# Attention scores in 64x64 array tiles on 48 stacked rows, and a step written out in slots

## The chip, the cores and the metric

The kernel runs on one core of a Trainium2 chip. The metric is the device time of one execution in microseconds (us), the median of several runs. The engines work from queues of their own and meet at semaphores: PE (TensorE, matrix products), DVE (VectorE), ACT (ScalarE), POOL (GpSimd) and SP (SyncE, which here only issues DMAs).

## The reference

One post-norm transformer layer in float32 on x of 8 batches, 256 tokens, 128 features: attention with 16 heads of 8 dimensions and a sliding window of 128 keys, then a layer norm, then a mixture of 8 experts of which each token takes its best 2, then a layer norm.

```python
q, k, v = (to_heads(a) for a in jnp.split(x @ w_qkv.T, 3, axis=-1))   # 16 heads of 8
att = jnp.einsum('bhqd,bhkd->bhqk', q, k) / sqrt(8)
att = where((j <= i) & (j >= i - 127), att, -inf);  att = softmax(att)
x = layernorm(x + (att @ v) @ w_out.T)
probs = softmax(x @ router_w);  top_p, top_e = top_k(probs, 2)
y = sum over the two experts e of top_p * (gelu(x @ w_in[e] + b_in[e]) @ w_out[e] + b_out[e])
x = layernorm(x + y)
```

## The kernel before

**Exact scores from bfloat16.** Queries and keys are projected in float32, one batch at a time (`project_qk`, L926), and each value is split into three bfloat16 parts. ACT copies the first part out of PSUM (`take_top`, L550); DVE takes the rest by subtraction, the middle part by a conversion and the last by another subtraction (`split_rest`, L671 to L676). SP writes the parts to memory and reads them back stacked on partitions (`write_parts`, `stack`), so that one bfloat16 product over 72 rows (9 products of parts, each of 8 dimensions) gives a score. A batch has two stacks of 8 heads each, and there are buffers for two batches.

**Two passes over the scores.** The first pass finds each row's largest score. In the first tile of 128 queries a mask goes into PSUM by a product with the identity (L942), then one product a head (L945). In the second tile, for 2 heads at a time, there is a mask (L955) and per head two products of 64 queries by 192 keys, in the two column halves of the array (L960). DVE takes the maxima (L743, L748). They are split into three parts (`split_max`, L685 to L691), turned on PE (L1001), copied by ACT (L482) and written by a DMA into three rows below the stacked queries, which makes 75 rows. The second pass (`turned_scores`, L977 and L978) gives the scores turned and with the maximum taken off: per head 256 and 128 columns. ACT takes the exponential of one head at a time out of one of two banks (L474), POOL masks (L432, L436), and PE weighs the values in four column tiles of 32 (`weigh_values`, L992, L994).

**What follows in a step.** The output is turned (L1008), divided by its sums (DVE L698, L706), turned (L1014), projected (L1020), added to x and normed (DVE), turned again (L1026), and gives router logits (L1032).

**The order.** It is written out by hand. `step` treats one batch's first pass together with the second pass of the batch before and the tail of the two before that, in four quarters `g` of four heads. A first stretch of steps and the last two are written out; the steps between run in a hardware loop (`Fori`), where addresses and semaphore values come from registers. The experts follow, in 4 chunks of 512 tokens: a first layer (L1043, three products of 512 columns), gelu on ACT (L574), a second layer (L1051), and DVE adds the share (L813). Their first units are interleaved with the last batch's attention.

## Time and profile before

| | us |
|---|---|
| median of 3 runs | 224.44 (224.05 to 225.66) |
| the profiled execution, its own time | 223.83 |
| its span in the trace | 221.8 |

The span is the time between the first and the last instruction of the trace; the profiled execution has 2.0 us outside it. On the page a group of instructions has its busy time and the mean duration of one. Matrix products are pipelined: two that follow each other start closer together than one lasts, so what a product costs its engine is read from the difference of two starts. An idle time is put down to what ended it.

### The profile page before, as it was taken

The page shows a single profiled execution, that of the slowest core. Times are in us where ns is not written, and L with a number is a line of the kernel's source. Part 1 is how long each engine was busy: PE and PEld are TensorE (multiplying, and loading weights), DVE is VectorE, ACT ScalarE, POOL GpSimd, SP SyncE. Part 2 cuts the span into 40 slices and gives each one's busy share as a digit, 9 for nine tenths or more (in the row PEclk, how much of TensorE's full clock was granted, in tenths as well). Part 3 has the DMA queues.
Part 4 walks back from the last instruction along what each step waited for, and adds up shares of the span by engine and source line. Part 5 has one row for each costly group of instructions (what it writes and reads, how often), then busy time and mean ns, then how long its engine had stood idle before and what let it go on. Part 6 is the DMA issues. An engine that isn't in the chain of part 4 may idle for free.

```text
span 221.8 us, 5963 instructions
## 1 busy us (share of the span) xinstructions
PE 203.4 (92%) x1906; PEld 135.9 (61%) x1908; DVE 182.9 (82%) x522; ACT 116.7 (53%) x270; POOL 89.2 (40%) x166
## 2 busy tenths in 40 slices
PE   7786999989999999999999999989999899999960
PEld 4332446555565565565566566656688798989950
DVE  6664655789979989989989998977899888988883
ACT  2200106647557557557557566769445756374530
POOL 7230003375445635635635536478244211422103
PEclk9997559999999999999999999999999999999996
DMA  4947751542633533533533431000000001000011
GB/s 113 282 117 240 202 148 46 151 147 77 170 120 104 163 110 99 162 104 99 160 104 99 158 104 29 5 26 3 0 4 0 0 3 45 7 24 24 3 47 47
DMA packets 20391, 19.66 MB, mean 89 GB/s; under 512 B 1609, under 2 KB 17937, under 8 KB 20369
## 3 DMA queue, kind: packets, MB, share of 16 engines
q1 hardware_dynamic: 20180, 19.30, 29.4%
q8 instruction: 12, 0.20, 0.4%
q14 instruction: 10, 0.08, 0.1%
q10 hardware_dynamic: 189, 0.09, 0.1%
HBM read 13.94 MB, written 5.24 MB: 86 GB/s over the span
## 4 chain that ended last, share of the span: by engine, by line
PE 63%; DVE 17%; issue 7%; ACT 4%; DMA 4%; POOL 1%; SPq 1%; DVEq 1%; POOLq 0%; ACTq 0%
PE bank L1051 12%; PE bank L1043 9%; PE bank L960 7%; PE bank L977 5%; PE bank L992 4%; PE bank L955 3%; PE bank L942 3%; PE bank L945 3%; PE bank L926 3%; PE bank L1089 3%; DMA ks<-k_scratch 2%; DVE rest L671 2%; DVE neg_max L748 2%; PE bank L978 2%; DVE parts L676 2%
## 5 line engine op out<-in xcount | busy, mean ns | idle before, releaser
L474 ACT ACTIVATE probs<-bank 128x384 f32<-128x384 f32 x128 | 60.0, 496 | 34.7 <-PE bank L978 32.5
L432 POOL TENSOR_SCALAR_AFFINE_SELECT probs<-probs 128x1024 f32<-128x1024 f32 x32 | 35.7, 1116 | 67.8 <-ACT probs L474 67.8
L813 DVE SCALAR_TENSOR_TENSOR x_rows<-bank,gate_c,x_rows 128x128 f32<-128x128 f32 (+1 forms) x128 | 36.6, 343 | 5.3 <-PE bank L1051 4.2
L748 DVE TENSOR_REDUCE neg_max<-bank 128x2 f32<-128x384 f32 x64 | 33.5, 546 | 3.4 <-PE bank L960 3.1
L1051 PE MATMUL bank<-w_out_sb,hid 128*128 128x128 f32 x256 | 34.2, 277 | 1.0 <-DVE x_rows L813 1.0
L1051 PEld LDWEIGHTS bank<-w_out_sb,hid 128*128 128x128 f32 x256 | 32.6, 191 | 3.4 <-DVE x_rows L813 1.4
L574 ACT ACTIVATE hid<-bank,b_in_sb 128x512 f32<-128x512 f32 x32 | 21.9, 687 | 22.4 <-PE bank L1043 22.3
L977 PE MATMUL bank<-qs,ks 75*128 75x256 bf16 x128 | 33.4, 279 | 0.1
L743 DVE TENSOR_REDUCE neg_max<-bank 128x4 f32<-128x512 f32 x32 | 21.9, 685 | 8.8 <-PE bank L945 8.1
L978 PE MATMUL bank<-qs,ks 75*128 75x128 bf16 x128 | 26.9, 218 | 0.0
L436 POOL TENSOR_SCALAR_AFFINE_SELECT probs<-probs 128x512 f32<-128x512 f32 x32 | 24.2, 756 | 0.0
L960 PE MATMUL bank<-ks,qs 72*64 72x192 bf16 x256 | 24.1, 271 | 0.0
L992 PE MATMUL bank<-probs,v 128*32 128x256 f32 x256 | 20.4, 391 | 0.0
L977 PEld LDWEIGHTS bank<-qs,ks 75*128 75x128 bf16 x128 | 12.8, 100 | 11.0 <-ACT probs L474 0.7
L955 PE MATMUL bank<-mask_second,ident_bf 128*128 128x256 bf16 x64 | 18.6, 290 | 0.8 <-DVE neg_max L748 0.3
L960 PEld LDWEIGHTS bank<-ks,qs 72*64 72x64 bf16 x256 | 9.3, 111 | 11.9 <-issue 10.3
L942 PE MATMUL bank<-mask_first,ident_bf 128*128 128x512 bf16 x32 | 13.2, 412 | 3.5 <-DMA ks<-k_scratch 3.5
L1089 PE MATMUL bank<-idle_rows 128*128 128x512 bf16 x50 | 14.6, 445 | 1.8 <-DVE idle_rows L791 1.4
L1043 PE MATMUL bank<-x_hi,w_in_lo 128*128 128x512 f32 (+1 forms) x32 | 15.3, 478 | 0.0
L563 ACT ACTIVATE v<-bank 128x64 f32<-128x64 f32 x32 | 4.6, 234 | 17.5 <-PE bank L932 17.5
L945 PEld LDWEIGHTS bank<-ks,qs 72*128 72x128 bf16 x128 | 10.6, 103 | 5.0 <-issue 1.4
L945 PE MATMUL bank<-ks,qs 72*128 72x128 bf16 x128 | 13.4, 231 | 0.0
(117 smaller groups left out, 343.8 us busy)
## 6 DMA issues: line engine op xcount, KB each, us to landing
qs<-q_scratch SPq DMA_DIRECT2D x16, 288.0 KB
ks<-k_scratch SPq DMA_DIRECT2D x16, 288.0 KB
q_scratch<-parts SPq DMA_DIRECT2D x8, 192.0 KB, 2.1
k_scratch<-parts SPq DMA_DIRECT2D x8, 192.0 KB, 2.4
x_cols<-x_t SPq DMA_DIRECT2D x8, 128.0 KB, 2.6
x_rows<-x SPq DMA_DIRECT2D x8, 128.0 KB, 2.2
k_scratch<-parts SPq DMA_DIRECT2D x8, 128.0 KB, 2.3
out<-y_sb SPq DMA_DIRECT2D x8, 128.0 KB, 1.8
```

Of the source, the lines that this page charges most:

```text
L432: pool.affine_select(out=own, in_=own, compare_op=ALU.is_ge, fill=0.0, base=0, pattern=[[0, 2], [0, 4], [1, P]], channel_multiplier=-1).th ...
L474: nc.scalar.activation(probs[g][:, :, i, :], st_banks(spare)[k % len(st_banks(spare))][:, 0:3 * P].rearrange("p (k c) -> p k c", k=3), ACT ...
L748: nc.vector.tensor_reduce(neg_max[:, 1, 4 * g + 2 * u:4 * g + 2 * u + 2], score_bank[1 + u][:, 0:384].rearrange("p (h c) -> p h c", h=2), ...
L813: nc.vector.scalar_tensor_tensor(token_rows(c, n), y_bank[e % 4][:, n * E:(n + 1) * E], gate_of(c, n, e), token_rows(c, n), ALU.mult, ALU. ...
L945: last = mm(score_bank[0][:, i * P:(i + 1) * P], q[0:ROWS, h, 0:P], k[0:ROWS, h, 0:P], start=False, stop=True, skip_group_check=True)
L955: mm(edges, ident_bf[:, :], mask_second[:, :, :].unsqueeze(1).to_broadcast([P, 2, 2, 64]), start=True, stop=True)
L960: last = mm(bank_u[lo:lo + 64, i * 192:(i + 1) * 192], q[0:ROWS, h, P + lo:P + lo + 64], k[0:ROWS, h, lo:lo + 192], start=False, stop=True ...
L977: mm(out_bank[:, 0:T], k[0:KROWS, h, 0:P], q[0:KROWS, h, :], start=True, stop=True)
L978: mm(out_bank[:, T:T + P], k[0:KROWS, h, P:T], q[0:KROWS, h, P:T], start=True, stop=True).then_inc(st_ready, 1)
L992: last = mm(o_bank[rows, t * T:(t + 1) * T], v, probs[g][:, 0:2, j, :], start=s == 0, stop=s == 1, skip_group_check=True)
L1043: last = mm(hid_bank[e % 2][:, :], w[:, e, :], xx[:, cols], start=i == 0, stop=i == 2)
L1051: last = mm(y_bank[e % 4][:, n * E:(n + 1) * E], hid[e % 2][:, n * P:(n + 1) * P], w_out_sb[:, e, :], start=True, stop=True)
```

## The change

**Scores.** Of the nine products of parts six are kept (`PRODUCTS`), so a score needs 48 rows. An even and an odd head now lie side by side, at partitions 0 and 64. Both passes use products of at most 64 rows and 64 output partitions. The four of one pair of heads (two heads, two halves of the queries or keys) lie in the four quarters of the array, and the two heads write to different banks. The masks are made in the same shape, four products to a job. The second pass does a pair of heads at once, into one buffer of two banks, and ACT takes one exponential of 768 columns for it (L417) where it took two of 384. The maxima of all 16 heads are split in one go, by two DVE instructions, turned in one go and written by two DMAs.

**Splitting.** The first part is taken off inside PSUM by a product with minus the identity (`subtract_top`); ACT makes the middle part (`take_middle`), DVE the last (`take_low`).

**Loads.** There are four stacks. The five writes of a batch go out as their parts are ready, and a batch is projected 14 slots ahead. All of x in rows comes in one load, and most of x in columns is loaded after the first two stacks.

**Order.** The loops are gone. A batch has 8 slots, in which the constants say which piece is done; 75 slots are written out for every engine.

```diff
-BLK = PARTS * D
-ROWS = PARTS * BLK
+PRODUCTS = ((0, 1), (0, 0), (0, 2), (1, 0), (1, 1), (2, 0))
+ROWS = len(PRODUCTS) * D
+KROWS = ROWS + PARTS
...
-LOAD_WARM_UP = 7
-WARM_UP = 34
+LOAD_WARM_UP = 8
+WARM_UP = 44
...
+STACKS = 4
+TURN_MAX, VALUES, S2, PV = 8, 12, 11, 15
+COPY_O, TURN_O, TURN_ATTN, PROJECT_OUT, TURN_X1, LOGITS = 22, 23, 25, 26, 30, 31
+PROJECT_QK = -14
+LAST_S1, LAST_S2 = 8 * B - 1, 8 * B - 1 + S2
+SCORE_JOBS = {0: (False, 0), 1: (True, 0), 2: (True, 2), 4: (False, 4), 5: (True, 4), 6: (True, 6)}
+JOBS = 2 * len(SCORE_JOBS)
...
-                q0, k0 = par * PARTS * E, par * (2 * PARTS - 1) * E
-                sp.wait_ge(part_low, b.times(1, 1))
-                sp.dma_start(q_scratch[q0:q0 + PARTS * E, :].rearrange("(a r) t -> r a t", a=PARTS),
-                             parts[par][:, :, 0, :]).then_inc(scratch_written[par], 16)
-                sp.dma_start(k_scratch[k0:k0 + PARTS * E, :].rearrange("(a r) t -> r a t", a=PARTS),
-                             parts[par][:, :, 1, :]).then_inc(scratch_written[par], 16)
-                sp.dma_start(k_scratch[k0 + PARTS * E:k0 + (2 * PARTS - 1) * E, :]
-                             .rearrange("(a r) t -> r a t", a=PARTS - 1),
-                             parts[par][:, 0:PARTS - 1, 1, :]).then_inc(scratch_written[par], 16)
...
+            def stack(b):
+                sp.wait_ge(scratch_written[b % 2], 80 * (b // 2 + 1))
+                if b >= STACKS:
+                    sp.wait_ge(st_ready, PAIRS * (b - STACKS + 1))
+                for i, operand in enumerate((qs, ks)):
+                    for r in range(2):
+                        sp.dma_start(operand[b % STACKS][64 * r:64 * r + ROWS, :, :],
+                                     scratch[b % 2, i, :, r, :].rearrange("a (n t) -> a n t", n=PAIRS)).then_inc(stacked[b % STACKS], 16)
+            def stack_max(b):
+                sp.wait_ge(max_copied, b + 1)
+                for r in range(2):
+                    sp.dma_start(qs[b % STACKS][64 * r + ROWS:64 * r + KROWS, :, :],
+                                 max_t[r * PARTS * PAIRS:(r + 1) * PARTS * PAIRS, :]).then_inc(max_stacked[b % STACKS], 16)
...
+            write_parts(0)
+            sp.wait_ge(ones_ready, 1)
+            stack(0)
+            write_parts(1)
             sp.wait_ge(ones_ready, 2)
+            stack(1)
+            sp.dma_start(x_t_sb[:, 2 * T:B * T], x_t[:, 2 * T:B * T]).then_inc(x_t_loaded[2], 16)
+            sp.dma_start(wout_sb[:, :], wout_t).then_inc(out_w_loaded, 16)
+            sp.dma_start(router_sb[:, :], router_w).then_inc(moe_w_loaded, 16)
+            sp.dma_start(b_in_sb[:, :], b_in_t).then_inc(moe_w_loaded, 16)
+            sp.dma_start(x_sb[:, :, :], x.rearrange("(n p) e -> p n e", p=P)).then_inc(x_loaded, 16)
+            sp.wait_ge(ones_ready, STACKS)
...
+            def exponentials(b, p):
+                g = p // 2
+                if p % 2 == 0 and b:
+                    act.wait_ge(pv_done, QUADS * (b - 1) + g + 1)
+                act.wait_ge(st_ready, PAIRS * b + p + 1)
+                two = slice(2 * (p % 2), 2 * (p % 2) + 2)
+                nc.scalar.activation(probs[g][:, :, two, :].rearrange("p k j c -> p j k c"),
+                                     st[:, :, 0:3 * P].rearrange("p j (k c) -> p j k c", k=3), ACT.Exp, scale=SCALE).then_inc(exp_done, 1)
...
+            def take_middle(b):
+                act.wait_ge(part_rest, b + 1)
+                nc.scalar.activation(parts[b % 2][:, 1, :, :], projection_bank(b)[:, :].rearrange("p (a t) -> p a t", a=2), ACT.Copy).then_inc(part_mid, 1)
...
+                for offset, piece in ((TURN_MAX, copy_max), (TURN_ATTN, copy_attention), (PROJECT_QK, take_top), (PROJECT_QK + 1, take_middle),
+                                      (VALUES, pad_v), (COPY_O, copy_output), (TURN_X1, copy_x1), (LOGITS, copy_logits)):
...
-            def split_rest(b, in_use=True):
-                p = parts[b.parity]
-                dve.wait_ge(part_top, b.times(1, 1))
-                if in_use:
-                    dve.wait_ge(part_low, b.times(1))
-                nc.vector.tensor_tensor(rest[:, :, :], misc[0][:, :].rearrange("p (a t) -> p a t", a=2), p[:, 0, :, :],
-                                        ALU.subtract).then_inc(part_rest, 1)
-                dve.wait_ge(part_rest, b.times(1, 1))
-                nc.vector.tensor_copy(p[:, 1, :, :], rest[:, :, :]).then_inc(part_mid, 1)
-                dve.wait_ge(part_mid, b.times(1, 1))
-                nc.vector.tensor_tensor(p[:, 2, :, :], rest[:, :, :], p[:, 1, :, :], ALU.subtract).then_inc(part_low, 1)
...
+            def take_low(b):
+                p = parts[b % 2]
+                dve.wait_ge(part_mid, b + 1)
+                nc.vector.tensor_tensor(p[:, 2, :, :], projection_bank(b)[:, :].rearrange("p (a t) -> p a t", a=2), p[:, 1, :, :],
+                                        ALU.subtract).then_inc(part_low, 1)
...
+            def split_max(b):
+                part = max_parts[b % 2]
+                upper = upper_half(part[:, :, :, :, :])
+                dve.wait_ge(maxima, JOBS * (b + 1))
+                nc.vector.tensor_tensor(part[:, :, :, 1, :], part[:, :, :, 0, :], upper[:, :, :, 0, :], ALU.subtract).then_inc(max_rested, 1)
+                dve.wait_ge(max_rested, b + 1)
+                nc.vector.tensor_tensor(part[:, :, :, 2, :], part[:, :, :, 1, :], upper[:, :, :, 1, :], ALU.subtract).then_inc(max_split, 1)
...
+                if slot == LAST_S1 + 1:
+                    split_weights()
+                    route_shift(EARLY, B // 2 - 1)
+                if slot == LAST_S1 + 2:
+                    choose(EARLY, 1)
...
+            def subtract_top(b):
+                pe.wait_ge(part_top, b + 1)
+                mm(projection_bank(b)[:, :], minus_bf[:, :], parts[b % 2][:, 0, :, :], start=False, stop=True, skip_group_check=True).then_inc(part_rest, 1)
...
+            def scores(b, second, pair, job):
+                q, k = qs[b % STACKS], ks[b % STACKS]
+                heads, width = (2, 192) if second else (4, P)
+                if job % JOBS == 0:
+                    pe.wait_ge(stacked[b % STACKS], 64 * (b // STACKS + 1))
+                for r in range(2):
+                    if job + r >= 3:
+                        pe.wait_ge(maxima, job + r - 2)
+                    bank = score_bank[(job + r) % 3][:, 0:heads * width].rearrange("p (h c) -> p h c", h=heads)
+                    rows = slice(64 * r, 64 * r + 64)
+                        cols = slice(64 * half, 64 * half + 64)
+                        if second:
+                            at = bank[cols, :, :].rearrange("p h (a c) -> p h a c", a=3)[:, :, 0:3:2, :]
+                            mask = edges[rows, 0:2, :].unsqueeze(1).to_broadcast([64, heads, 2, 64])
+                        elif half:
+                            at = bank[cols, :, 64:P]
+                            mask = edges[rows, 1, :].unsqueeze(1).to_broadcast([64, heads, 64])
+                        else:
+                            at = bank[cols, :, :]
+                            mask = edges[rows, 1:3, :].rearrange("p a c -> p (a c)").unsqueeze(1).to_broadcast([64, heads, P])
+                        mm(at, ident_bf[rows, 64 * r:64 * r + 64], mask, start=True, stop=True)
+                for i in range(heads):
+                    for r in range(2):
+                        rows = slice(64 * r, 64 * r + ROWS)
+                        bank = score_bank[(job + r) % 3]
+                        for half in range(2):
+                            lo = 64 * half
+                            if second:
+                                keys, queries = slice(lo, lo + 192), slice(P + lo, P + lo + 64)
+                            else:
+                                keys, queries = slice(0, 64 + lo), slice(lo, lo + 64)
+                            last = mm(bank[lo:lo + 64, i * width:i * width + keys.stop - keys.start], q[rows, pair + i, queries], k[rows, pair + i, keys],
+                                      start=False, stop=True, skip_group_check=True)
+                        if i == heads - 1:
+                            last.then_inc(scores_ready, 1)
...
+            def turned_scores(b, p):
+                q, k = qs[b % STACKS], ks[b % STACKS]
+                if p == 0:
+                    pe.wait_ge(max_stacked[b % STACKS], 32 * (b // STACKS + 1))
+                if b or p:
+                    pe.wait_ge(exp_done, PAIRS * b + p)
+                for kt in range(2):
+                    for half in range(2):
+                        for r in range(2):
+                            rows, cols = slice(64 * r, 64 * r + KROWS), slice(64 * half, 64 * half + 64)
+                            at = kt * P + 64 * half
+                            last = mm(st[cols, r, kt * T:kt * P + T], k[rows, p, at:at + 64], q[rows, p, kt * P:T], start=True, stop=True)
+                last.then_inc(st_ready, 1)
...
+            for slot in range(LAST_S2 + 1):
+                n = pair_at(slot)
+                if n is not None:
+                    turned_scores(*n)
+                elif slot < S2:
+                    keep_warm(2)
+                n = jobs_at(slot)
+                if n is not None:
+                    scores(*n)
...
+                b = batch_at(slot, PROJECT_QK)
+                if b is not None:
+                    if b == 2:
+                        pe.wait_ge(x_t_loaded[2], 16)
+                        pe.wait_ge(part_low, 2)
+                    elif b < 5:
+                        pe.wait_ge(max_copied, b - 2)
+                    else:
+                        pe.wait_ge(attn_copied, b - 4)
+                    project_qk(b)
+                b = batch_at(slot, PROJECT_QK + 1)
+                if b is not None:
+                    subtract_top(b)
```

The places where the order of the instructions matters here are two. On PE in the loop, at the start of a quarter (`bank` is a bank of PSUM, `qs` and `ks` the stacked queries and keys), there stood before:

```order
L941 REGISTER_ALU
L942 MATMUL bank<-mask_first,ident_bf 128x512
L945 MATMUL bank<-ks,qs 128x128 x4
L975 REGISTER_ALU
L977 MATMUL bank<-qs,ks 128x256
L978 MATMUL bank<-qs,ks 128x128
L953 REGISTER_ALU
L955 MATMUL bank<-mask_second,ident_bf 128x2x2x64
L960 MATMUL bank<-ks,qs 64x192 x4
```

Now a slot of the steady part (the third of a batch) reads, up to the projections that follow:

```order
L938 MATMUL st<-qs,ks 64x256 [waits exp_done]
L938 MATMUL st<-qs,ks 64x256 x3
L938 MATMUL st<-qs,ks 64x128 x4
L910 MATMUL score_bank<-edges,ident_bf 64x2x2x64 [waits maxima]
L910 MATMUL score_bank<-edges,ident_bf 64x2x2x64
L910 MATMUL score_bank<-edges,ident_bf 64x2x2x64 [waits maxima]
L910 MATMUL score_bank<-edges,ident_bf 64x2x2x64
L921 MATMUL score_bank<-ks,qs 64x192 x8
L997 MATMUL misc<-wout_sb,attn_t 128x128 [waits attn_copied]
L997 MATMUL misc<-wout_sb,attn_t 128x128
L868 MATMUL misc<-x_t_sb,wqkv_sb 128x256 [waits attn_copied]
L868 MATMUL misc<-x_t_sb,wqkv_sb 128x256
```

The turned scores moved to the head of the slot; they come as eight small products behind one wait for the exponential of the pair before, and the projections follow behind waits for ACT. On SP at the start (`x_t` is x in columns, with 1536 columns for the batches from the third on) there stood before:

```order
L286 DMA b_in_sb<-b_in_t 128x8
L287 DMA x_t_sb<-x_t 128x1536
L290 DMA b_out_rows<-b_out 24x1x128 x3
L248 DMA q_scratch<-parts 128x3x256
L250 DMA k_scratch<-parts 128x3x256
L252 DMA k_scratch<-parts 128x2x256
L266 DMA qs<-q_scratch 72x1x2048
L266 DMA ks<-k_scratch 72x1x2048
```

Now, from the second batch's last write on:

```order
L228 DMA scratch<-parts 128x2x256 [waits part_low]
L238 DMA qs<-scratch 48x2048 [waits scratch_written1,ones_ready]
L238 DMA qs<-scratch 48x2048
L238 DMA ks<-scratch 48x2048 x2
L261 DMA x_t_sb<-x_t 128x1536
L262 DMA wout_sb<-wout_t 128x128
L263 DMA router_sb<-router_w 128x8
L264 DMA b_in_sb<-b_in_t 128x8
L265 DMA x_rows<-x 128x16x128
L212 DMA scratch<-parts 128x3x256 [waits part_top,stacked0,ones_ready]
```

The load of the 1536 columns moved behind the writes and the stacks of two batches.

## Rows read from the trace of the kernel before

**Rows 1.** Page, busy us with share of the span, and count, of each engine.

```profile
PE 203.4 (92%) x1906; PEld 135.9 (61%) x1908; DVE 182.9 (82%) x522; ACT 116.7 (53%) x270; POOL 89.2 (40%) x166
```

**Rows 2.** Stretches of 10 us: busy (count) of each engine, clock, DMA share, GB/s.

```profile
20.00:30.00 10.00, 9.67 (x57) 4.49 (x57) 6.38 (x15) 0.95 (x5) 0.00 (x0) 0.50 0.56 159
...
100.00:110.00 10.00, 9.64 (x118) 5.78 (x116) 9.64 (x23) 6.46 (x18) 5.98 (x8) 1.00 0.43 127
```

**Rows 3.** Page, the chain that ended last: its shares by engine.

```profile
PE 63%; DVE 17%; issue 7%; ACT 4%; DMA 4%; POOL 1%; SPq 1%; DVEq 1%; POOLq 0%; ACTq 0%
```

**Rows 4.** Timeline (start us, us, engine, line, op): TensorE around two heads' scores.

```profile
88.79 0.38 PE L942 MATMUL bank<-mask_first,ident_bf 128*128 128x512 bf16 x1
...
89.01 0.39 PE L945 MATMUL bank<-ks,qs 72*128 72x128 bf16 x4
...
89.23 0.27 PE L977 MATMUL bank<-qs,ks 75*128 75x256 bf16 x1
...
89.40 0.27 PE L955 MATMUL bank<-mask_second,ident_bf 128*128 128x256 bf16 x1
...
89.60 0.36 PE L960 MATMUL bank<-ks,qs 72*64 72x192 bf16 x4
...
89.89 0.28 PE L977 MATMUL bank<-qs,ks 75*128 75x256 bf16 x1
```

**Rows 5.** Timeline, TensorE, and a group (mean ns): weighing the values, and what follows.

```profile
91.31 0.42 PE L992 MATMUL bank<-probs,v 128*32 128x256 f32 x4
...
L992 PE MATMUL bank<-probs,v 128*32 128x256 f32 x256 | 20.4, 391 | 0.0
...
129.13 0.40 PE L994 MATMUL bank<-probs,v 128*32 128x128 f32 x8
129.46 0.71 PE L1020 MATMUL bank<-wout_sb,attn_t 128*128 128x128 f32 x4
```

**Rows 6.** Groups by line and shape (count, busy us, mean ns, idle before): VectorE and ScalarE.

```profile
L474 ACT ACTIVATE probs<-bank 128x384 f32<-128x384 f32 x128 | 60.0, 496 | 34.7 <-PE bank L978 32.5
...
L748 DVE TENSOR_REDUCE neg_max<-bank 128x2 f32<-128x384 f32 x64 | 33.5, 546 | 3.4 <-PE bank L960 3.1
...
L743 DVE TENSOR_REDUCE neg_max<-bank 128x4 f32<-128x512 f32 x32 | 21.9, 685 | 8.8 <-PE bank L945 8.1
...
L676 DVE TENSOR_TENSOR parts<-rest,parts 128x512 bf16<-128x512 f32 x8 | 10.4, 1302 | 0.3
...
L691 DVE TENSOR_TENSOR max_parts<-max_rest,max_parts 128x16 bf16<-128x16 f32 x16 | 8.0, 497 | 0.5
...
L685 DVE CAST max_parts<-neg_max 128x16 bf16<-128x16 f32 x16 | 6.0, 374 | 0.7
...
L550 ACT ACTIVATE parts<-bank 128x512 bf16<-128x512 f32 x8 | 4.8, 597 | 8.7 <-PE bank L926 8.7
```

**Rows 7.** Timeline: two projections of queries and keys, four rounds apart.

```profile
34.26 1.08 PE L926 MATMUL bank<-x_t_sb,wqkv_sb 128*128 128x256 f32 x4
...
98.15 1.08 PE L926 MATMUL bank<-x_t_sb,wqkv_sb 128*128 x4
```

**Rows 8.** Timeline and DMA issues (KB each, median us to landing): the start.

```profile
13.91 0.78 SPq L266 DMA_DIRECT2D ks<-k_scratch  x1
...
18.79 0.39 PE L942 MATMUL bank<-mask_first,ident_bf 128*128 128x512 bf16 x1 [2.76 <-DMA ks<-k_scratch]
...
33.42 0.27 PE L977 MATMUL bank<-qs,ks 75*128 75x256 bf16 x1
...
q_scratch<-parts SPq DMA_DIRECT2D x8, 192.0 KB, 2.1
...
x_t_sb<-x_t SPq DMA_DIRECT2D x1, 768.0 KB, 5.8
```

**Rows 9.** Timeline, and group: the first second layer, and the splitting of the weights.

```profile
157.64 1.16 PE L1051 MATMUL bank<-w_out_sb,hid 128*128 128x128 f32 x8
...
L788 DVE TENSOR_TENSOR w_in_lo<-w_in_sb,w_in_hi 128x1024 fp32r<-128x1024 f32 x1 | 2.0, 1995 | 0.0
```

1154 lines of the change are left out of this document (490 added, 664 removed).

## The prediction

> **What bounds the kernel now.** I read the page's busy times first, then the stretches, the chain of waits, and last the timeline of one quarter of a step. TensorE is busy 92% of the span and VectorE 82% [rows 1]. In the stretches of 10 us in mid-attention TensorE is busy 9.64 and VectorE 9.64, ScalarE 6.46 [rows 2]. So the two lie side by side; the chain has 63% on PE and 17% on DVE [rows 3]. Four rounds of the loop lie between the projections at 34.26 and 98.15 [rows 7], so one step, which is one batch, takes (98.15 - 34.26) / 4 = 16.0 us. I cut the time at three points: the first turned scores at 33.42 [rows 8], the first second layer at 157.64 [rows 9], and the end at 221.8. That makes 33.4, 124.2 and 64.2 us.
>
> **TensorE per batch.** Costs are differences of starts [rows 4]. A first tile of 4 heads takes 89.23 - 88.79 = 0.44, a head's turned scores 89.40 - 89.23 = 0.17, a second tile of 2 heads 89.89 - 89.40 = 0.49. Scores cost 4 x 0.44 + 16 x 0.17 + 8 x 0.49 = 8.4 of the 16.0 us, and all else 7.6. In the second tile the mask's 256 columns need 0.11 at 2.4 GHz and start 0.20 before the products of half width; these need 2 x 192 columns, 0.16, when halves run together, and start 0.29 before the next. So there are 0.09 and 0.13 us at each change of tile shape. Behind the values, whose last 128 columns pass four times in float32, each of two pairs of passes 0.11, it is 129.46 - 129.13 - 0.21 = 0.12 [rows 5]. I take 0.11.
>
> After the change four small products share the array. The trace shows column tiles together: four weighings of 256 columns start within 0.42 - 0.39 = 0.03 us of each other [rows 5]. Row halves together it does not show. Bounds: fully together, a pair's turned scores take 256 + 128 columns = 0.16; not at all, 0.32. I take 0.16, nearest to the column tiles. A first job of 8 heads is 512 columns of mask and 4 x 128, 0.43; a second job of 4 heads 256 + 2 x 192, 0.27. Per batch: 8 x 0.16 + 2 x 0.43 + 4 x 0.27 = 3.2 where 8.4 stood. The subtraction adds 512 columns, 0.21. Projections, turns and values now each leave the 64x64 shape and return: some 18 changes a batch, of which 8 stood around the values and are in the 7.6; 10 x 0.11 = 1.1 more. TensorE's own work: 7.6 + 3.2 + 0.2 + 1.1 = 12.1 us.
>
> The Trainium skill has a rule against such small products (TensorE: Matmul & The Clock Gate, on the gap of two matmuls: "Start-to-start never drops below ≈25 ns however small N is"). The row has four starts in 0.03 us, 10 ns each or less, and speaks against it; with 25 ns the time would be that of the fourth rival.
>
> **VectorE per batch.** It has 0.96 x 16.0 = 15.4 us [rows 2]. The maxima stay: 8 x 0.52 and 4 x 0.69 [rows 6]. Of the three splitting instructions the 1.30 of L676 goes, and another conversion that I leave uncounted. Splitting the maxima took 8 instructions a batch, the first kind 0.37 and the last 0.50 in the mean [rows 6], so 8 x 0.44 = 3.5; now 2 of at most twice that, 0.9. Left: 15.4 - 1.3 - 2.6 = 11.5.
>
> **ScalarE per batch.** 384 columns take 0.50 and 512 take 0.60 [rows 6], 0.8 ns a column, so 768 take 0.82: 6.6 for 8 where 16 x 0.47 = 7.5 stood. The middle part adds 0.60. ScalarE had 0.65 x 16 = 10.3 and has 10.0.
>
> **Why a batch won't take 12.1.** There is one buffer for turned scores: PE may write a pair only when the exponential of the pair before is done. I walked one batch on paper, slot by slot, with these durations and 0.3 from a product's start to its reader. A slot whose TensorE work is short waits for the exponential: turned scores 0.11 + 0.37, exponential 0.82, 0.1 back, 1.4 us, which costs 0.4 in the first slot. With three score banks PE waits for VectorE in three slots, 0.2, 0.3 and 0.5. The subtraction stands one slot behind the projection, and ScalarE's copy (0.60 and 0.3 to reach it) is hidden only by the turned scores: 0.7. The logits wait for a copy behind an exponential and the copy of the output: 0.8. Sum 2.9; about 0.7 of waiting was in the 7.6. So 12.1 + 2.2 = **14.3 us** a batch, against 16.0.
>
> **The start.** First scores come at 18.79 now [rows 8]. Afterwards 46 warm-up products replace 34 and end near 19, about when the first stack is there. Slots 0 to 2 end near 22. Then `project_qk` of the third batch needs the 1536 columns. Their load follows five writes, four reads of 0.78 each to issue, five writes and four reads. The first set is written by 10, landed 2.1 later [rows 8], the reads issued by 15.3; second writes by 18, landed near 20.4, reads issued by 24; then the load, 768 KB, which took 5.8 to land beside others [rows 8]. It can do with 4: **28.5**. PE idles 6 us. Before, TensorE stood still before 18.79 and the stretch from 20 to 30 has clock 0.50, the 1.2 GHz level [rows 2]; I expect it again here. From 28.5: projection 1.8 at that level, copy 0.7, warm-up products and subtraction 1.2, copy 0.7, last part 0.8 with its issue, landing 2.5: 36.4. Four reads to issue, 3.2; behind them on SP the two writes of the first batch's maxima, 1.6, and landing 2: the first turned scores at **43.3**, not 33.4. That is 9.9 lost. If the load takes 5.8 it is 2 more; if 2.5, 1.5 less.
>
> **The middle.** Slots 11 to 15: 5 x 1.4 = 7. Slots 16 to 63, six batches: 85.8. The last two of these have no projection (0.91 + 0.32 + 0.7 of waiting, 3.9 for both), and the first has no tail yet, where turns, logits and their wait would be 2; I take off 5, as VectorE takes over in part. Slots 64 to 74: TensorE light, bound by the exponential round of 1.4 to 1.5, 16. The splitting of the expert weights now stands there: 2.0 [rows 9], the part before it, and routing, for which ScalarE waits in its order and behind it the exponentials; then `choose`, behind which the residual of the sixth batch waits and PE with it. 2.7 more. Then 1.3 to the first second layer. Sum 7.0 + 85.8 - 5.0 + 18.7 + 1.3 = **107.8**, not 124.2. VectorE's small instructions lie between 0.37 and 0.50 for 16 columns, as other work meets them; add 1.5.
>
> **The end.** The experts' products and shares are the same; the loops go, which PE at 99% busy did not show as a cost. 64.2 stays, between -1 and +2 for the routing of the second half, which now stands in the second chunk.
>
> **Sum.** 43.3 + 109.3 + 64.2 = 216.8, and 2.0 outside the span: **219 us**, against 223.83 of the profiled execution, which lies 0.6 below the median of 224.44.
>
> **The rivals.**
> 1. *VectorE alone is the bound.* If the waits of my walk overlap, a batch takes VectorE's 11.5 and some 1 of gaps. 12.5: 6 x 1.8 = 11 less, 208. For it: TensorE has slack of a slot. Against: one buffer of turned scores. 0.20.
> 2. *The maxima's write comes late every batch* (slower). Turned, copied by ScalarE 1.7 into slot 8, issued by 3.3, landed by 5.4; slot 11 starts at 5.2. It decides from a landing of 2.1 up. The first stack's read needed 18.79 - 14.69 = 4.1 after its issue [rows 8], and the maxima stand in one queue behind such reads. 2 us more in six and a half batches, 13: 232. 0.16.
> 3. *Row halves don't run together.* 8 x 0.16 + 2 x 0.43 + 4 x 0.27 = 3.2 more on PE, some 2.3 of it not hidden, in 7.5 batches: 236. The change then doesn't do what it says. 0.12.
> 4. *A floor between starts.* A product of 128 columns now takes 0.22 / 4 = 55 ns of L945's time [rows 4]. If starts came no closer than half of that, 27 ns (an estimate), a pair's 8 turned products would take 0.22 and not 0.16, a first job's 16 scores 0.43 and not 0.21, a second job's 8 0.22 and not 0.16: 0.06 x 8 + 0.22 x 2 + 0.06 x 4 = 1.2 a batch, some 0.8 of it not hidden, 6 us: 225. The skill's figure above is nearly this case. 0.05.
> 5. *Loss and gain cancel*: 15 us a batch and a start 2 us later, 225. 0.08.
>
> My forecast keeps 0.39. A measurement of this kernel tells about 1% from no change, 222.2 to 226.7. Faster 0.58, of the forecast and the first rival with a little taken off; same 0.14; slower 0.28 with the second and third. The range: from 207, which takes in the first rival, to 232, with the second; the third and the low edge of the first stay out. The forecast's own range is 214 to 223.
>
> **What would show it.** Steps: products of one pair in the four quarters start within 0.03 us and a pair's turned scores take 0.16; a batch takes 14.3 in mid-attention; PE waits for the load of x in columns until 28.5; the first turned scores at 43. Wrong if that load lands before slot 2 ends, if the waits before a batch's first turned scores end in a DMA, or if TensorE's clock falls again in the steady part.

## The result, and the profile after

The changed kernel takes 227.06 us (median of 7 runs, 225.65 to 228.44), the kernel before, run beside it, 225.49. The ratio is 1.0084, interval 1.0048 to 1.0121: 0.8% slower. 219 was forecast, as a gain. Unedited beside later experiments it came to 1.0183 (1.0124 to 1.0242). Its profiled execution took 225.65, with a span of 223.8. TensorE's clock is low for longer in some executions of a kernel than in others, and the ratios leave out executions of the edited kernel that took over 1.5% more than its fastest, while the medians keep them.

On the page TensorE and VectorE are both less busy than in [rows 1], and the time is not shorter:

```profile
PE 184.1 (82%) x2402; PEld 125.8 (56%) x2402; DVE 152.7 (68%) x454; ACT 110.2 (49%) x206; POOL 80.9 (36%) x155
...
PEclk9999769769999999999999998556999999999996
```

The clock's row shows where to look: it falls at the start (slices 5 to 9) and again in slices 25 to 28. The stretches of 10 us say it with numbers (columns as in [rows 2]):

```profile
20.00:30.00 10.00, 4.25 (x27) 2.08 (x22) 2.16 (x5) 0.60 (x1) 0.00 (x0) 0.77 0.91 249
...
110.00:120.00 10.00, 8.02 (x178) 5.40 (x170) 8.88 (x22) 6.65 (x15) 7.24 (x10) 1.00 0.01 2
120.00:130.00 10.00, 8.10 (x170) 5.43 (x166) 7.96 (x20) 6.22 (x14) 6.06 (x9) 1.00 0.02 6
130.00:140.00 10.00, 5.61 (x98) 3.18 (x91) 8.98 (x30) 4.73 (x8) 2.66 (x2) 0.90 0.01 3
140.00:150.00 10.00, 7.62 (x70) 4.07 (x69) 4.17 (x12) 3.86 (x10) 5.92 (x8) 0.50 0.01 2
```

From 130 to 140 TensorE does 5.6 us and VectorE 9.0; then TensorE has the 1.2 GHz level. This is the drain, slots 64 to 74, where no first pass is left.

The timeline of TensorE, ScalarE and of SP's issues gives the start, to be read beside [rows 8]:

```profile
21.23 0.43 SPq L261 DMA_DIRECT2D x_t_sb<-x_t  x1
...
26.94 2.08 PE L868 MATMUL misc<-x_t_sb,wqkv_sb 128*128 128x256 f32 x4 [5.75 <-DMA x_t_sb<-x_t]
...
34.71 0.89 SPq L238 DMA_DIRECT2D ks<-scratch  x2
36.09 0.38 ACT L437 ACTIVATE max_t<-misc 48x256 bf16<-48x256 bf16 x1 [5.14 <-PE misc L969]
36.49 1.61 SPq L245 DMA_DIRECT2D qs<-max_t  x2
...
39.91 0.36 PE L938 MATMUL st<-qs,ks 51*64 51x256 bf16 x8 [0.75 <-DMA qs<-max_t]
```

The third batch's projection waited 5.75 us for the load of x in columns, and the first turned scores come at 39.91, 6.5 us later than before. SP wrote the first batch's maxima (L245) as soon as ScalarE had copied them, at 36.47. The last reads of the third stack, which stand ahead of them on SP, had been issued by 35.60. So two paths end here within 0.9 us: the late load with the work behind it, and SP's queue. In mid-attention the parts cost what was forecast, or a little more:

```profile
103.85 0.36 PE L938 MATMUL st<-qs,ks 51*64 51x256 bf16 x8
104.03 0.38 PE L910 MATMUL score_bank<-edges,ident_bf 64*64 64x512 bf16 x4
104.16 0.39 PE L921 MATMUL score_bank<-ks,qs 48*64 48x128 bf16 x16
104.47 0.29 PE L969 MATMUL misc<-ident_bf,max_parts 128*48 128x128 bf16 x2
...
107.14 0.28 PE L910 MATMUL score_bank<-edges,ident_bf 64*64 64x256 bf16 x4
107.26 0.34 PE L921 MATMUL score_bank<-ks,qs 48*64 48x192 bf16 x8
107.52 0.71 PE L997 MATMUL misc<-wout_sb,attn_t 128*128 128x128 f32 x4
```

A pair's turned scores take 104.03 - 103.85 = 0.18 (0.16 forecast), a first job 0.44 (0.43), a second job 0.38 (0.27). The 0.11 that a second job has more is what the forecast had apart for a change of tile shape. The exponentials of slots 19 and 67, the first pairs of two batches six apart, start at 54.60 and 136.22, so a batch takes 13.6 us, 14.3 forecast, 16.0 before. Where TensorE stands still in mid-attention, over the four batches from 67.44 to 122.16 (total us, times, longest):

```profile
PE score_bank L910 <- DVE max_parts L623: 2.1, 3, 0.7
PE st L938 <- ACT probs L417: 1.9, 6, 0.4
PE misc L875 <- ACT parts L425: 1.2, 3, 0.4
PE misc L1013 <- ACT x_t L472: 1.1, 4, 0.4
PE o_bank L954 <- POOL probs L378: 1.0, 1, 1.0
```

The first four are the four waits of the forecast's walk: the score banks, the exponential, the subtraction and the logits. All five come to 7.3 / 4 = 1.8 us a batch.

Three times cut each run below: the first exponential, the exponential of slot 64, and the first second layer. For the kernel after they are 40.3, 131.0 and 158.6; the last is [rows 9]'s 157.64 before. The drain took 27.6 us. What held it is on the timeline of VectorE, with a row each of GpSimd and TensorE:

```profile
131.98 2.07 DVE L696 TENSOR_TENSOR w_in_lo<-w_in_sb,w_in_hi 128x1024 fp32r<-128x1024 f32 x1
...
134.94 0.22 DVE L596 TENSOR_REDUCE row_stat<-route 128x8 f32<-128x64 f32 x1 [0.32 <-ACT route L483]
...
138.78 0.22 DVE L604 TENSOR_TENSOR gate<-route 128x64 f32<-128x64 f32 x1
139.04 0.42 DVE L661 TENSOR_TENSOR resid<-misc,x_rows 128x256 f32<-128x256 f32 x1
...
140.36 0.22 POOL L368 TENSOR_SCALAR var_eps<-moments 128x2 f32<-128x2 f32 x1 [5.81 <-DVE moments L674]
...
143.06 1.08 PE L954 MATMUL o_bank<-probs,v 128*32 128x256 f32 x8 [1.85 <-POOL probs L378]
```

and in the list of waits from 130 to 158 (total us, times, longest):

```profile
ACT probs L417 <- PE st L938: 11.6, 8, 3.0
POOL var_eps L368 <- DVE moments L674: 10.3, 2, 5.8
...
PE misc L885 <- DVE resid L661: 2.1, 1, 2.1
```

The residual of the sixth batch (L661) stands behind the 16 small instructions of `choose` (L596 to L604). Behind it wait TensorE's `project_v` (L885) and GpSimd's deviation (L368), and in GpSimd's queue the masks (L376, L378) behind that, for which TensorE waits before it weighs the values; the exponentials wait for TensorE.

### The profile page after: what moved, and what is told of

Its sections match the earlier page's. It is cut to its first block and busy times, and to the rows that moved or that the text cites. A ratio compares the mean times of both kernels' runs of the same rounds, so it can differ in the third digit from the quotient of the medians.

```text
span 223.8 us, 6039 instructions
## 1 busy us (share of the span) xinstructions
PE 184.1 (82%) x2402; PEld 125.8 (56%) x2402; DVE 152.7 (68%) x454; ACT 110.2 (49%) x206; POOL 80.9 (36%) x155
## 3 DMA queue, kind: packets, MB, share of 16 engines
q1 hardware_dynamic: 21281, 17.29, 28.8%
## 5 line engine op out<-in xcount | busy, mean ns | idle before, releaser
L417 ACT ACTIVATE probs<-st 128x768 f32<-128x768 f32 x64 | 52.1, 814 | 37.0 <-PE st L938 36.8
L376 POOL TENSOR_SCALAR_AFFINE_SELECT probs<-probs 128x1024 f32<-128x1024 f32 x32 | 35.0, 1093 | 64.4 <-ACT probs L417 64.4
L623 DVE TENSOR_REDUCE max_parts<-score_bank 128x2 f32<-128x384 f32 x64 | 32.5, 549 | 6.2 <-PE score_bank L921 5.9
L938 PE MATMUL st<-qs,ks 51*64 51x256 bf16 (+1 forms) x512 | 24.8, 272 | 10.9 <-ACT probs L417 8.0
L507 ACT ACTIVATE hid<-score_bank,b_in_sb 128x512 f32<-128x512 f32 x32 | 21.9, 687 | 21.1 <-PE score_bank L1023 21.0
L626 DVE TENSOR_REDUCE max_parts<-score_bank 128x4 f32<-128x512 f32 x32 | 20.6, 685 | 11.0 <-PE score_bank L921 10.8
L954 PE MATMUL o_bank<-probs,v 128*32 128x256 f32 x256 | 22.2, 421 | 4.4 <-POOL probs L378 4.4
L611 DVE TENSOR_TENSOR parts<-misc,parts 128x512 bf16<-128x512 f32 x8 | 5.5, 691 | 23.8 <-ACT parts L430 23.8
L862 PE MATMUL o_bank<-idle_rows 128*128 128x512 bf16 x74 | 20.6, 422 | 1.2 <-DVE idle_rows L702 1.2
L378 POOL TENSOR_SCALAR_AFFINE_SELECT probs<-probs 128x512 f32<-128x512 f32 x32 | 21.3, 665 | 0.0
L910 PE MATMUL score_bank<-edges,ident_bf 64*64 64x256 bf16 (+1 forms) x192 | 19.4, 311 | 2.1 <-DVE max_parts L623 2.1
L921 PE MATMUL score_bank<-ks,qs 48*64 48x192 bf16 (+2 forms) x512 | 20.1, 232 | 0.0
L746 DVE SCALAR_TENSOR_TENSOR x_rows<-st,gate,x_rows 128x128 f32<-128x128 f32 x64 | 18.0, 342 | 2.4 <-PE st L1037 2.0
L368 POOL TENSOR_SCALAR var_eps<-moments 128x2 f32<-128x2 f32 x8 | 1.7, 217 | 34.9 <-DVE moments L674 34.9
```

What stands on the lines that cost most here:

```text
L376: pool.affine_select(out=own, in_=own, compare_op=ALU.is_ge, fill=0.0, base=0, pattern=[[0, 2], [0, 4], [1, P]], channel_multiplier=-1).th ...
L378: pool.affine_select(out=other, in_=other, compare_op=ALU.is_gt, fill=0.0, base=0, pattern=[[0, 4], [-1, P]], channel_multiplier=1).then_i ...
L417: nc.scalar.activation(probs[g][:, :, two, :].rearrange("p k j c -> p j k c"), st[:, :, 0:3 * P].rearrange("p j (k c) -> p j k c", k=3), A ...
L507: nc.scalar.activation(hid[e % 2][:, :], hid_bank[e % 2], ACT.Gelu_apprx_tanh, bias=b_in_sb[:, e:e + 1]).then_inc(gelu_done, 1)
L623: nc.vector.tensor_reduce(top[:, 1, r, pair:pair + 2], bank[:, 0:384].rearrange("p (h c) -> p h c", h=2), X_AXIS, ALU.max, negate=True).th ...
L626: nc.vector.tensor_reduce(top[:, 0, r, pair:pair + 4], bank[:, :].rearrange("p (h c) -> p h c", h=4), X_AXIS, ALU.max, negate=True).then_i ...
```

## The experiments

All edit the changed kernel, but for the last, b_warm. "Start" is the first exponential, "drain" the time from the exponential of slot 64 to the first second layer, both from the profiled execution; the ratio is to the kernel before on the same chip. A stage is read from one profiled execution of each kernel. The time from the first exponential to slot 64 shows how far such executions differ: 90.7 us in the changed kernel's, 93.2 in e_route's, whose edit stands behind that stretch. The medians of neighbours differ as well (227.06 and 229.39 for the unedited kernel), so the stages are compared beside the ratios.

| run | start | drain | median us | ratio (interval) |
|---|---|---|---|---|
| after | 40.3 | 27.6 | 227.06 | 1.0084 (1.0048 to 1.0121) |
| c_after | 42.1 | 27.8 | 229.39 | 1.0183 (1.0124 to 1.0242) |
| e_weights | 40.6 | 26.7 | 228.95 | 1.0192 (1.0146 to 1.0238) |
| e_route | 42.6 | 23.9 | 225.46 (223.09 of those in the ratio) | 0.9908 (0.9859 to 0.9957) |
| e_both | 40.6 | 23.4 | 225.12 (its four shortest 220.92 to 223.33) | before 224.95; no interval |
| e_warm | 41.3 | 28.4 | 228.26 | 1.0124 (1.0069 to 1.0179) |
| e_both_warm | 41.6 | 20.9 | 222.04 | 0.9821 (0.9760 to 0.9882) |
| e_xsplit | 39.5 | 27.9 | 227.68 | 1.0101 (1.0059 to 1.0143) |
| e_both_xsplit | 40.0 | 22.2 | 221.13 | 0.9786 (0.9725 to 0.9847) |
| e_order | 33.8 | 28.2 | 226.20 | 1.0025 (0.9988 to 1.0063) |
| e_both_order | 33.9 | 23.8 | 221.44 | 0.9829 (0.9774 to 0.9884) |
| e_all | 33.2 | 20.9 | 218.99 | 0.9724 (0.9660 to 0.9789) |
| e_order2 | 33.7 | 28.1 | 218.93 | 0.9657 (0.9612 to 0.9702) |
| e_order2_late | 33.1 | 27.6 | 216.83 | 0.9624 (0.9578 to 0.9671) |
| e_best | 32.9 | 20.9 | 212.45 | 0.9381 (0.9335 to 0.9426) |
| e_apart | 40.7 | 28.3 | 227.23 | 1.0042 (1.0004 to 1.0081) |
| b_warm | | | 220.43 (219.97 of those in the ratio) | 0.9768 (0.9711 to 0.9826) |

### The drain: VectorE's work, and the clock

```diff
+                if slot == 18:
+                    split_weights()
...
-                    split_weights()
```

> The changed kernel with one edit: VectorE splits the expert weights in slot 18, in a gap of 3.75 us before a take_low, and not in slot 64. Theory A (VectorE's work in slots 64 and 65, weights 2.7 us and routing 5.1 us, holds the residual of batch 5, behind it TensorE, and the idle TensorE then loses its clock): the chain is 2.7 us shorter, and more if the clock falls later: 222 to 225 against 227.1, the stretch 140 to 150 still below clock 0.8. Theory B (the drain is slow because only one pair's turned scores fit the buffer and TensorE has too little work there, so its clock falls whatever VectorE does): within 1 us of the changed kernel, 226 to 228, clock as before.

Measured: drain 0.9 us shorter, no gain in the ratio; 228.95 lies above the ranges of both theories. What the weights held is one round: from the exponential of slot 65 to that of slot 66 it took 2.48 us, as ScalarE's routing exponential (L483) stands ahead of the second, and now 1.39. The weights alone are not the drain's loss: ScalarE's routing exponentials and `choose` come earlier, and the residual is still behind them.

```diff
-                if slot == LAST_S1 + 2:
+                if slot == 69:
                     choose(EARLY, 1)
```

> The changed kernel with one edit: choose(EARLY), 17 small VectorE instructions of 4.1 us, stands in slot 69 behind the first norm of batch 5, and not in slot 65 ahead of its residual. Theory A: the residual, the deviation on GpSimd and the masks queued behind it no longer wait; 3 to 6 us less, 221 to 224, and the granted clock from 140 to 150 above 0.7. Theory B: within 1 us, 226 to 228, the clock from 140 to 150 at 0.5.

Measured: drain 23.9, 3.7 us shorter; the residual is the main part. But the clock fell all the same, at 146, so theory A's "above 0.7" held from 140 to 150 (0.84) only because the fall came later. Its time, 225.46, lies above theory A's 221 to 224, and 223.09 without the longest executions inside it.

> Both edits: weights split in slot 18, choose(EARLY) in slot 69. Theory A: the time from the turned scores of slot 64 to the first second layer falls from 28 us to about 20, as the prediction had it: 218 to 221, and TensorE's clock stays above 0.9 through the drain. Theory B: 225 to 228, the clock falls as before.

Measured: drain 23.4, not 20, and 225.12 where theory A wanted 218 to 221. So theory A explains 4.2 us of the drain and no more. In the stretches of 4 us of this run (busy, count, clock) TensorE is less idle and the clock falls nevertheless, as theory B said:

```profile
134.00:138.00 4.00, 2.82 (x48) 1.00 0.01 4
138.00:142.00 4.00, 2.68 (x47) 0.94 0.02 4
142.00:146.00 4.00, 3.08 (x33) 0.50 0.00 0
```

Products on idle rows, alone:

```diff
+                if 65 <= slot <= 74:
...
+                    for _ in range(2):
+                        mm(score_bank[2][:, :], idle_rows[:, 0:P], idle_rows[:, :], start=True, stop=True)
```

> The changed kernel with two products of 512 columns on idle rows at the end of each of slots 65 to 74, into a score bank that is free by then; nothing else moves. If the fall of the clock to 0.5 in the drain costs by itself, and not only the stall: the clock from 140 to 150 stays at 0.9 or more and the time falls by 3 to 6 us, 221 to 224 (theory B wants the upper gain, since the clock is then the whole loss; theory A at most 4 us, since VectorE's 7 us of work still hold the chain, and slots 64 to 66 stay long). If the clock's fall costs nothing on the path: 227 to 230, the products themselves being 0.43 us a slot.

Measured: no gain, drain 28.4, and the clock fell too, though later and for 10 us, not 17. The added products stand in TensorE's own queue, so while it waits for VectorE they wait with it:

```profile
138.00:142.00 4.00, 2.21 (x28) 1.00 0.00 0
142.00:146.00 4.00, 1.89 (x26) 0.65 0.02 4
```

With the stall gone and the products from slot 64 on:

> The changed kernel with three edits: weights split in slot 18, choose(EARLY) in slot 69, and two products of 512 columns on idle rows at the end of each of slots 64 to 74. With the two VectorE edits alone the clock still fell, at 141, to 0.50 for 14 us, though TensorE was busy 0.7 and more. If the added products hold the clock (theory: low TensorE work in the drain is what drops it): clock 1.0 from 130 to 160, first second layer at about 151 and the time 4 to 6 us below the changed kernel with the two edits, 217 to 220 where its starts are alike. If the clock falls all the same: no gain, 225 to 228.

Measured: 1.0 throughout, drain 20.9:

```profile
134.00:138.00 4.00, 4.00 (x59) 1.00 0.03 8
138.00:142.00 4.00, 3.65 (x50) 1.00 0.02 4
142.00:146.00 4.00, 3.48 (x46) 1.00 0.00 0
146.00:150.00 4.00, 3.62 (x43) 1.00 0.00 0
```

The drain is 23.4 - 20.9 = 2.5 us shorter. The same pair with the other start, e_both_order and e_all below, gives 23.8 - 20.9 = 2.9. e_both_xsplit below has the same edits of the drain as e_both but a clock that was low for 10 us and not 14, and gives 22.2 - 20.9 = 1.3. The time, 222.04, is above the 217 to 220 that was expected, and so is the first second layer (153.6, not 151).

These differences are what is left after the added products have been paid for. The seven rounds from the exponential of slot 64 to that of slot 71 lie ahead of the clock's fall in e_both and take 10.0 us there, and 11.1 in e_both_warm. From slot 71 to the first second layer it is 13.4 and 9.8. So the fall cost e_both at least 3.6. Products that nothing ahead of them stalls held the clock; in e_warm, where something did, they didn't.

At 2.4 GHz throughout, two rounds of the drain are still long (e_both_warm):

```profile
143.79 0.83 ACT L417 ACTIVATE probs<-st 128x768 f32<-128x768 f32 x1
146.74 0.81 ACT L417 ACTIVATE probs<-st 128x768 f32<-128x768 f32 x1 [1.94 <-PE st L939]
148.08 0.81 ACT L417 ACTIVATE probs<-st 128x768 f32<-128x768 f32 x1 [0.52 <-PE st L939]
149.31 0.58 PE L1024 MATMUL score_bank<-x_hi,w_in_lo 128*128 128x512 f32 x1
150.70 0.81 ACT L417 ACTIVATE probs<-st 128x768 f32<-128x768 f32 x1 [1.54 <-PE st L939]
```

Rounds 71 to 72 and 73 to 74 take 2.95 and 2.62 us. In the first TensorE has the logits, the turned output, the values and the added products ahead of the next turned scores, in the second the first expert's first layer, which runs until 150.29.

> The changed kernel unedited, beside which the others of this set are read on one chip: 226 to 228, with the clock's fall of some 14 us in the drain from about 138 on.

Measured: 229.39, above its range, its load landing 1.8 us later than in the first profile (projection at 28.78). So much can the unedited kernel differ from one set of runs to another.

### The start: SP's order

e_xsplit loads x for the third batch early:

```diff
+            sp.dma_start(x_t_sb[:, 2 * T:3 * T], x_t[:, 2 * T:3 * T]).then_inc(x_t_loaded[2], 16)
...
-            sp.dma_start(x_t_sb[:, 2 * T:B * T], x_t[:, 2 * T:B * T]).then_inc(x_t_loaded[2], 16)
+            sp.dma_start(x_t_sb[:, 3 * T:B * T], x_t[:, 3 * T:B * T]).then_inc(x_t_loaded[3], 16)
```

> The changed kernel with one edit: the 128 KB of x in columns for the third batch are loaded as the third load at the start, the other 640 KB where the 768 KB stood. Theory S (the wait of 5.75 us before the third projection, which ends when the 768 KB land, moves the first turned scores back one for one, and costs the clock at the start as well): projection at 21 and not 26.9, first turned scores at 34 to 36 and not 39.9, the time 4 to 6 us shorter, 221 to 223. Rival: the path of writes, reads and maxima on SP's one queue is what ends last; then the first turned scores come at 38 or later and the time falls by less than 2 us, 225 to 227.

Measured: the projection came at 20.84, but the first turned scores at 38.95. Theory S fell and the rival held, though the time, 227.68, is 0.7 above its range. The timeline (SP's issues, ScalarE, TensorE) names what ends last:

```profile
28.42 0.38 ACT L438 ACTIVATE max_t<-misc 48x256 bf16<-48x256 bf16 x1 [4.74 <-PE misc L970]
...
28.59 0.49 SPq L228 DMA_DIRECT2D scratch<-parts  x1
...
33.20 0.89 SPq L238 DMA_DIRECT2D ks<-scratch  x2
34.13 1.62 SPq L245 DMA_DIRECT2D qs<-max_t  x2
...
38.95 0.54 PE L939 MATMUL st<-qs,ks 51*64 51x256 bf16 x8 [7.45 <-DMA qs<-max_t]
```

The maxima are copied at 28.8 and issued at 34.1, behind the reads of the third stack, which wait until the third batch's parts have landed and are wanted only in slot 16, five slots after the maxima. In the changed kernel the load's path ended last, 0.9 us behind this one, so mending the load alone uncovered it.

> The changed kernel with the weights split in slot 18, choose(EARLY) in slot 69 and the load of x for the third batch split off and early. If start and drain add up: 4 to 6 us of the start and 2 to 5 of the drain, 217 to 220, clearly below the kernel before. If only the drain counts: 222 to 225. If neither: 226 to 228.

Measured: 221.13, ratio 0.9786, between the first two of its cases. What it gains is in the drain (22.2); the start is 40.0.

e_order has the same load and writes the first batch's maxima ahead of the third stack's reads:

```diff
-                if b is not None:
+                if b:
                     stack_max(b)
...
+                if slot == 5:
+                    stack_max(0)
                 b = batch_at(slot, PROJECT_QK + 3)
```

> The changed kernel with the load of x for the third batch split off and early, and one more edit: on SP the two writes of the first batch's maxima stand ahead of the four reads of the third stack, not behind them. With the load alone the maxima were copied at 28.8, but SP issued them at 34.1, behind reads that wait for the third batch's parts, and they landed at 38.9. If SP's order is what ends last: first turned scores at 32 to 35, no fall of the clock between 30 and 42, and the time 4 to 7 us below the changed kernel: 221 to 224. If the landing of small writes behind large reads is the bound whatever the order: 37 or later, 226 to 228.

Measured: first turned scores at 33.35, as wanted, and 226.20, above its 221 to 224. SP's order without the early load was not tried. There these writes would stand behind those of the third batch's parts, which wait for the load. The gain was given back one batch later:

```profile
52.41 0.54 PE L941 MATMUL st<-qs,ks 51*64 51x256 bf16 x8 [8.09 <-DMA qs<-max_t]
```

The second batch's maxima stand behind the fourth stack's reads in the same way (SP issued these at 45.70 and the maxima at 47.46).

> The same start (x split, maxima ahead of the third stack's reads), with the weights split in slot 18 and choose(EARLY) in slot 69. If start and drain are what the forecast missed, both come to its 33 to 43 and 20 us: 216 to 219. If the gain at the start is given back in a wait for the second batch's maxima: 220 to 222.

> All edits: x split, maxima ahead of the third stack's reads, weights split in slot 18, choose(EARLY) in slot 69, and two products on idle rows at the end of each of slots 64 to 74. If the clock's fall in the drain costs by itself as well: 2 to 4 us below the same kernel without the added products, 213 to 216. If it doesn't: the same or 1 us more.

Measured: 221.44 for the first, its second case (220 to 222): TensorE waits 6.04 us for the second maxima. The second took 218.99, which is 2.4 us below, as its drain is 2.9 shorter; it misses its 213 to 216 and has the same wait for the maxima, 6.47 us.

e_order2 keeps the early load and moves every batch's reads behind the maxima of the batch two before:

```diff
                     stack_max(b)
+                    if b + 2 < B:
+                        stack(b + 2)
...
-                b = batch_at(slot, PROJECT_QK + 3)
-                if b is not None:
-                    stack(b)
```

> The changed kernel with the load of x for the third batch split off and early, and on SP every batch's maxima written ahead of the four reads of the stack two batches later. If SP's order holds back the second batch's maxima: TensorE's wait for them, 8.1 us with only the first batch's order changed, is under 3 us, and the time 4 to 7 us below the changed kernel of the same chip, 220 to 223. If it is the traffic: the wait stays at 5 us or more, 224 to 227.

Measured: 218.93, ratio 0.9657, below its 220 to 223; the wait fell from 8.09 to 1.20, and the clock is 1.0 from 20 to 50:

```profile
45.41 0.36 PE L938 MATMUL st<-qs,ks 51*64 51x256 bf16 x8 [1.20 <-DMA qs<-max_t]
...
30.00:40.00 10.00, 6.92 (x134) 4.10 (x137) 6.83 (x13) 5.58 (x11) 3.19 (x4) 1.00 0.84 204
```

With only an early load and SP's order, and the drain untouched, the change is a gain of 3.4% over the kernel before as it was. SP's order was the cause of the second batch's wait, and not the traffic.

> The same, and the loads of x in rows and of the expert weights, 2 MB in all, are issued in slots 17, 19 and 23 and not ahead of slot 10. If the traffic of these loads slows the writes of the parts (5.3 us to issue four, against 2.0 for the first batch) and the landing of the maxima: 2 to 4 us below the kernel with SP's order alone. If not: the same within 1 us.

Measured: 216.83 against 218.93, and the intervals of the two ratios overlap (0.9624 and 0.9657). Whether the traffic costs anything more stays open, though it shows in SP's issues (last section).

> All of it: the start of the two kernels above, weights split in slot 34, choose(EARLY) in slot 69, two products on idle rows at the end of each of slots 64 to 74. The forecast's own steps with a start of 33 to 35, six and a half batches at 13.6, a drain of 20 and the end of 64 give 33 + 7 + 82 + 20 + 65 + 2 = 209. 208 to 213 if they add up; 215 or more if a further wait takes the place of those removed.

Measured: 212.45, ratio 0.9381, the fastest of all, at the top of its range. Start 32.9 and drain 20.9 are as wanted. From slot 19 to slot 64, though, it took 124.36 - 44.03 = 80.3 us, and the changed kernel 131.00 - 54.60 = 76.4: 3.9 more. e_order2_late, which differs from it by the three edits of the drain alone, took 77.8. Of the 2.5 between these two, a wait for maxima has 1.1 (2.17 us at 58.61, and 1.07 there). In the rest the weights' splitting stands now in the steady part, and the clock fell once for 3.4 us; what share each has was not tried.

### The row halves, and the kernel before

```diff
-                for i in range(heads):
-                    for r in range(2):
+                for r in range(2):
+                    for i in range(heads):
```

and likewise in the turned scores.

> The changed kernel with one edit: in the scores of a job and in the turned scores of a pair all products of the upper 64 rows come first, then all of the lower 64, so that only two quarters of the array can work at a time. If row halves work together in the changed kernel and are what brings the batch from 16.0 to about 13.6 us: a pair's turned scores take 0.32 and not 0.16, TensorE has some 2 us more work a batch, of which 1 to 2 are not hidden: 8 to 15 us more than the changed kernel, 235 to 243. If the batch is bound by the round of the exponential and TensorE's order doesn't matter: 227 to 230.

Measured: 227.23, ratio 1.0042, no slower than the changed kernel, as the second case had it, but not for its reason. The first case was wrong in its premise. In this run a pair's turned scores still take 100.27 - 100.08 = 0.19, and a first job's 16 scores 98.00 - 97.55 = 0.45, where 104.47 - 104.16 = 0.31 stood:

```profile
97.55 0.52 PE L921 MATMUL score_bank<-ks,qs 48*64 48x128 bf16 x16
98.00 0.71 PE L885 MATMUL misc<-wqkv_sb,x_t_sb 128*128 128x128 f32 x4
...
100.08 0.37 PE L938 MATMUL st<-qs,ks 51*64 51x256 bf16 x8
100.27 0.27 PE L910 MATMUL score_bank<-edges,ident_bf 64*64 64x256 bf16 x2
```

So the edit adds some 0.3 us a batch, not 2, and hiding 0.3 us says little. What it shows is that issuing one row half after the other hardly parts them. It doesn't show what the kernel would be without the overlap. How the 2.4 us that a batch gains divide among the parts of the change (fewer rows, quarters, one exponential a pair, no loops) was not tried either.

```diff
-WARM_UP = 34
+WARM_UP = 46
```

> The kernel before with one edit: 46 warm-up products of 512 columns where 34 stood, so that TensorE does not stand still from 16.0 to 18.8 ahead of its first scores. It shows what the clock's fall from 19 to 33 costs the kernel before, and so what a fair rival of the others is. If TensorE's clock bounds that stretch: clock 1.0 from 20 to 40 and 3 to 5 us less, 220 to 222. If DMA bounds it: 224 to 226.

Measured: 220.43, ratio 0.9768. Its runs at a mean clock of 0.99 took 219.6 to 220.4, those at 0.96 to 0.98 took 223.2 to 225.0. So the clock's fall at the start, in [rows 2], cost the kernel before some 4 us. That is read from the mean clocks: the profiled execution is the slowest of the seven, with a clock of 0.57 from 20 to 30, so the added products kept the clock in four executions of seven. Against this mended kernel before, e_best is still 3.6% faster (212.45 to 220.43), and e_order2, with 218.93, only 0.7%.

## Why the prediction was wrong

**The step that failed is the drain**, "Slots 64 to 74: ... 16", with 2.7 and 1.3 behind it: 20.0, where the exponential of slot 64 to the first second layer took 27.6. Three things make up the 7.6 that are missing: 1.5, 2.5 and 3.6.

- *The hold, 2.7 forecast, 4.2 measured.* I had named the residual, `choose` and TensorE behind them. I had left out that GpSimd's masks queue behind the deviation that waits for the same residual. Moving VectorE's work away took 4.2 us off.
- *The clock, which the sum had at nothing.* With no first pass TensorE is busy for 2.7 to 2.8 of 4 us (e_both), the clock goes to the 1.2 GHz level for 14 us, and for 17 in the changed kernel. Holding it took 2.5 us off (1.3 and 2.9 in the two other comparisons), after the added products had been paid for. "Wrong if TensorE's clock falls again in the steady part" looked for it in the wrong place.
- *The walk itself.* Without its hold it is 16 + 1.3 = 17.3. With the hold gone and the clock held the drain is 20.9, 3.6 more. The added products have 1.1 of that in the first seven rounds; the rest is in two rounds of 2.95 and 2.62 us. I had 1.4 to 1.5 for every round and didn't count that the tail of batch 6 and the first expert's first layer stand in these two.

**The start** was forecast at 43.3 and came at 39.9. The items of that sum come to 43.0, as those from 28.5 on make 36.2 and not 36.4. The load landed at 26.9, not 28.5, by two errors that partly cancel: it was issued at 21.2, not 24.5, and took 5.7 us to land, not 4. What follows took 13.0 us and not 14.8. The loss was real and the place right, and in the changed kernel the load is what ended last. But the forecast had one path, and there are two. "Behind them on SP the two writes of the maxima" is the other, and it ended 0.9 us before the first: e_xsplit shows that the load alone gives next to nothing back, and e_order and e_order2 that the load and SP's order together do.

**The steady part** was right in its mechanism as far as the trace shows it; no experiment took it apart. A batch takes 13.6 and not 14.3. TensorE's scores cost 8 x 0.18 + 2 x 0.44 + 4 x 0.38 = 3.8 a batch where I had 3.2, and 0.4 of the difference is changes of tile shape, which I had in another term. The four waits of the walk are there, but TensorE's waits come to 1.8 us a batch and not 2.9. From the first turned scores to slot 64 it was 90.7 us, where the forecast's terms give 7.0 + 85.8 - 5.0 + 1.5 = 89.3.

**The end** took 223.8 - 158.6 = 65.2, within the range given for 64.2.

The balance: -3.4 at the start, +1.4 in the steady part, +7.6 in the drain, +1.0 at the end, 6.6 in all. 219 and 6.6 make 225.6, and the profiled execution took 225.65. The start's error went the other way by luck: with a right start the forecast would have been 215.6, and 10 off.

**The rivals.** VectorE alone is not the bound (13.6, not 12.5; it is busy 8.0 to 8.9 of 10). The maxima's write came late, but for the first two batches and not each: 0.75 and 1.95 us of wait, and 8.09 for the second when the start alone was moved forward. The floor between starts did not decide: 16 products of a first job take 0.31, 19 ns each. The Trainium skill (TensorE: Matmul & The Clock Gate, section "Wait — 56ns, not 53.3ns?") has 25 ns as the least distance of two starts. The trace does not agree: products in different quarters of the array go below it here. The fourth and the fifth rival gave the time, 225, by other terms; the fifth had 15 us a batch.

## What to carry over

A stretch that ends a pipeline needs a walk of its own, for every engine's queue: what is moved there because the engines are emptier can hold the one chain that is left. Look there for TensorE's clock too. Products that were to keep it up did so here only where nothing ahead of them in TensorE's queue stalled, and they have a price of their own. Where a wait is removed and nothing is gained, look for a second path that ended just ahead of it. On a queue that issues in order, put the small transfer that is wanted now ahead of a large one that waits for something and is wanted later, and then look at the next batch, where the same wait returns.

## What the runs showed of the hardware

- Eight turned products of 51 rows and 64 columns of the array, in its four quarters, take 0.18 to 0.19 us up to the next group's start, 24 ns each, and the 16 of a first job (48 rows) 0.31, 19 ns each. Ordering them by row half left the first as it was and made the second 0.45.
- Where products of 64x64 tiles are followed by others of the full array, 0.11 us came on top of their columns (a second job 0.38, where its 640 columns make 0.27 at 2.4 GHz).
- TensorE's clock fell to the 1.2 GHz level while it was busy 2.7 to 2.8 us of 4, in products of small tiles (e_both), and stayed at 2.4 GHz with 3.5 to 4.0 of 4, two products of 512 columns and 128 rows a slot among them (e_both_warm).
- SP took 2.0 us to issue four writes of a batch's parts for the first batch (e_xsplit), and 5.3 for the fourth in e_order, right behind the two loads of 512 KB; the first of the four alone took 3.1. In e_order2_late, where these loads come later, it took 2.1 for the fourth and 5.1 for the fifth, which is now behind one of them.
